# One transpose in place of four: the router's logits and its combine weights in an attention and mixture-of-experts kernel

## What is computed

```
x = x + softmax(mask((ln(x) Wq + bq) (ctx Wk + bk)^T / sqrt(d))) (ctx Wv + bv)
t = ln(x)
scores  = sigmoid(l2norm(t) @ l2norm(gate_w).T)          # 16 logits per token
combine = the 8 largest scores of a token, divided by their sum, 0 elsewhere
routed  = sum over e of combine[:, e] * (silu(t Wg[e]) * (t Wu[e])) Wd[e]
x = x + routed + (silu(t sWg) * (t sWu)) sWd
```

## Time and profile before

| | us |
|---|---|
| three runs | 704.92, 705.00, 705.68 |
| median | 705.0 |
| the profiled execution | 705.73 |
| its span from the first to the last instruction | 703.6 |
| PE busy | 685.5 (97%) |
| PE weight loads busy | 592.4 (84%) |
| DVE, ACT, POOL busy | 461.6, 239.8, 263.0 |

### The profile page before, as it was taken

How to read it: one execution, slowest core, us unless ns; L and a number is a source line. 1 busy time by engine, 2 the same in 40 slices (tenths; PEclk the granted TensorE clock), 3 DMA queues, 4 the chain that set the end, 5 groups by cost and what they waited for, 6 DMA issues and landing times.

```text
span 703.6 us, 10934 instructions
## 1 busy us (share of the span) xinstructions
PE 685.5 (97%) x3995; PEld 592.4 (84%) x3995; DVE 461.6 (66%) x1029; ACT 239.8 (34%) x485; POOL 263.0 (37%) x222
## 2 busy tenths in 40 slices
PE   8997899999999999999999999999999999999997
PEld 6575688888888888888898889888888888888886
DVE  4777656677677766667576766767576775775444
ACT  4545233333424233333323233233333334232221
POOL 2120532534342532525343432525343442434332
PEclk9998799999999999999999999999999999999999
DMA  6326411042110510033110410114100510005100
GB/s 188 113 68 180 157 40 60 1 121 92 61 31 0 182 61 36 26 87 126 60 31 1 182 61 31 30 60 153 61 31 1 182 60 31 2 23 190 61 0 31
DMA packets 32763, 51.18 MB, mean 73 GB/s; under 512 B 3918, under 2 KB 24391, under 8 KB 32711
## 3 DMA queue, kind: packets, MB, share of 16 engines
q1 hardware_dynamic: 32455, 50.23, 21.8%
q10 hardware_dynamic: 256, 0.26, 0.2%
HBM read 46.03 MB, written 4.46 MB: 72 GB/s over the span
## 4 chain that ended last, share of the span: by engine, by line
PE 89%; DVE 3%; DMA 2%; ACT 2%; issue 1%; SPq 1%; POOL 0%; POOLq 0%; DVEq 0%
PE y_ps L295 9%; PE y_ps L297 9%; PE y_ps L296 9%; PE gate_ps L295 9%; PE up_ps L295 9%; PE gate_ps L297 9%; PE gate_ps L296 9%; PE up_ps L297 9%; PE up_ps L296 9%; PE f_ps L383 2%; PE f_ps L405 1%; PE f_ps L416 1%; DMA cb<-c_rows 1%; DMA xin<-in_x_dram 1%; PE up_ps L304 1%
## 5 line engine op out<-in xcount | busy, mean ns | idle before, releaser
L1157 POOL TENSOR_TENSOR hidden<-hidden,cb 128x512 f32<-128x512 f32 x128 | 200.5, 1567 | 300.5 <-DVE hidden L950 250.6
L946 DVE SCALAR_TENSOR_TENSOR hidden<-hidden,gate_ps 128x512 f32<-128x512 f32 x136 | 93.1, 685 | 148.2 <-ACT hidden L663 147.9
L663 ACT ACTIVATE hidden<-gate_ps 128x512 f32<-128x512 f32 x136 | 81.4, 599 | 271.1 <-PE gate_ps L297 271.1
L295 PE MATMUL y_ps<-W,hs 128*128 128x256 f32 x544 | 156.9, 288 | 6.4 <-ACT hs L670 3.3
L297 PE MATMUL y_ps<-W,hs 128*128 128x256 f32 x544 | 153.9, 283 | 0.0
L296 PE MATMUL y_ps<-W,hs 128*128 128x256 f32 x544 | 153.7, 283 | 0.0
L956 DVE TENSOR_TENSOR hs<-hidden,hs 128x512 fp32r<-128x512 f32 x136 | 97.9, 719 | 27.3 <-ACT hs L670 27.3
L295 PEld LDWEIGHTS y_ps<-W,hs 128*128 128x128 f32 x544 | 102.9, 189 | 12.0 <-ACT hs L670 4.7
L295 PE MATMUL gate_ps<-xT,W 128*128 128x512 f32 x272 | 109.1, 401 | 0.0
L295 PE MATMUL up_ps<-xT,W 128*128 128x512 f32 x272 | 108.8, 400 | 0.0
L297 PE MATMUL gate_ps<-xT,W 128*128 128x512 f32 x272 | 108.6, 399 | 0.0
(11 more groups left out here) (141 smaller groups left out, 721.1 us busy)
## 6 DMA issues: line engine op xcount, KB each, us to landing
cb<-c_rows SPq DMA_DIRECT2D x64, 512.0 KB, 4.2
xin<-in_x_dram SPq DMA_DIRECT2D x8, 512.0 KB, 3.6
out_dram<-x SPq DMA_DIRECT2D x7, 512.0 KB, 7.0
stage<-in_L_ffn_w_gate_dram SPq DMA_DIRECT2D x16, 128.0 KB, 2.2
stage<-in_L_ffn_w_up_dram SPq DMA_DIRECT2D x16, 128.0 KB, 2.4
stage<-in_L_ffn_w_down_dram SPq DMA_DIRECT2D x16, 128.0 KB, 2.6
cb<-in_ctx_dram SPq DMA_DIRECT2D x1, 512.0 KB
out_dram<-x SPq DMA_DIRECT2D x2, 256.0 KB, 2.1
```

The source lines that it names most:

```text
L295: mm(ps, lh, rh, start=first and i == 0, stop=False)
L663: af(ew[:, i, :], gate_ps[i][:], ACT.Tanh, scale=0.5).then_inc(tanh_done, 1)
L946: V_.scalar_tensor_tensor(out=ew[:, i, :], in0=ew[:, i, :], scalar=1.0, in1=gate_ps[i][:], op0=ALU.add, op1=ALU.mult).then_inc(silu_done, 1)
L1157: pg.tensor_tensor(h[:, i, :], ew[:, i, :], cb[:, pair % PLACES, (e - 1) % 2, :], ALU.mult) \
```

## The change

The partition count is used in full. `zT` becomes 128 partitions wide. ACT reads the logits with four copies, each of 32 partitions by 128 columns, which put the four token tiles under each other on the partitions; then one transpose of 128 by 128 turns all four, and the result has the same layout as before. The combine weights, 128 tokens by 64 columns (tile, expert), are turned by one transpose into 64 partitions by 128 tokens; one copy of that shape takes them to SBUF, and the store writes 64 pieces of 128 numbers (512 bytes) in place of 16 rows of 512 numbers, so that `c_rows` in DRAM holds what it held.

```diff
-    assert HALF <= 512 and CT * D + 2 * KD * CKEYS + D <= PLACES * 2 * TOK
+    assert 2 * E * TILES == P and HALF <= 512 and CT * D + 2 * KD * CKEYS + D <= PLACES * 2 * TOK
...
-        zT = sb("zT", [2 * E, TOK])
+        zT = sb("zT", [TILES * 2 * E, D])
...
             def turn_z(b, hf):
                 wait_apart(pe, (z_read, upto(b, hf, 1, 1)))
-                for j in range(TILES):
-                    ins = nc.tensor.transpose(f_ps[0][:, j * 2 * E:(j + 1) * 2 * E], zT[:, j * P:(j + 1) * P],
-                                              ident[0:2 * E, 0:2 * E])
-                ins.then_inc(z_turned, 1)
+                nc.tensor.transpose(f_ps[0][:, 0:TILES * 2 * E], zT[:, 0:P], ident[:]).then_inc(z_turned, 1)

             def turn_c(b, hf):
                 pe.wait_ge(combined, upto(b, hf, 1, 1))
-                for j in range(TILES):
-                    ins = nc.tensor.transpose(f_ps[1][0:E, j * P:(j + 1) * P], cw[:, j, :], ident[:])
-                ins.then_inc(c_turned, 1)
+                nc.tensor.transpose(f_ps[1][0:TILES * E, 0:P], cw.rearrange("p j e -> p (j e)"), ident[:]) \
+                    .then_inc(c_turned, 1)
...
             def read_z(b, hf):
                 act.wait_ge(routed_z, upto(b, hf, 1, 1))
-                af(zT[:], f_ps[0][0:2 * E, :], ACT.Copy).then_inc(z_read, 1)
+                for j in range(TILES):
+                    ins = af(zT[j * 2 * E:(j + 1) * 2 * E, 0:P], f_ps[0][0:2 * E, j * P:(j + 1) * P], ACT.Copy)
+                ins.then_inc(z_read, 1)
...
-                af(cT[0:E, :], f_ps[1][0:E, :], ACT.Copy).then_inc(c_read, 1)
+                af(cT[0:TILES * E, 0:P], f_ps[1][0:TILES * E, 0:P], ACT.Copy).then_inc(c_read, 1)
...
-                act.dma_start(c_rows, cT[0:E, :]).then_inc(c_stored, 16)
+                act.dma_start(c_rows.rearrange("e (j t) -> j e t", j=TILES), cT[0:TILES * E, 0:P]) \
+                    .then_inc(c_stored, 16)
```

## The result

The changed kernel took 700.68 us in the median of 19 runs (697.11 to 710.34), the kernel before 708.10 in the median of 19 beside it (702.83 to 714.62). The ratio is 0.990, with a 95% interval from 0.987 to 0.993: faster, by 5 to 9 us. The profiled execution has a span of 697.5 us, against 703.6 before.

What follows compares the result with a forecast made beforehand. The prediction took PE to bound the loop: 7 x (0.45 + 0.31) = 5.3 us saved, less 0.2 in the start-up, makes 5.1, taking the median of 705.0 to 699.9. The range was 699.0 to 702.7.

Steps and rivals of the forecast that it cites:

- the sum: Whole kernel: 7 x (0.45 + 0.31) = 5.3 us saved, 0.2 given back in the start-up, so 5.1.
- What bounds the kernel: Loop: PE is never idle, 80.14 us per chunk period; what leaves its stream shortens the kernel seven times.
- turn_z: Logits turn on PE: one transpose at 0.11 us replaces a block of 0.56; saves 0.45 per chunk, bounds 0.21 and 0.48.
- turn_c: Combine-weights turn on PE: one transpose at 0.11 us replaces 0.42; saves 0.31 per chunk, bounds 0.29 and 0.34.
- read_z: ACT's logits read: four copies take 0.75 us for 0.59; 0.2 more taken, at most 0.49, paid in the start-up.
- The cover of read_z: Loop: copies end at 137.97, latest 138.26, before the logits transpose can start at about 138.3; hidden by 0.3 or barely.
- The turn of the weights: Wait of the weights transpose for DVE's weights: cover shrinks from 0.54 to 0.09 us, -0.1 at worst; taken as just covered.
- The store: Store of the turned combine weights: 64 pieces land in 1.6 to 2.1 us, 0.5 more at most, inside a cover of 1.4.
- The rival on the slower side: Store of combine weights lands late, past the 1.4 us cover, and PE waits at expert 1's down; 708.3 if 4.2; chance 0.05.
- The entry price stays: Rival at the logits turn: the 0.24 us belongs to its wait or change to transpose; 0.21 saved there, 701.6; chance 0.13.
- PE gets nothing: Rival at both turns: a single transpose between matmuls costs as much as four; 705.2 us; chance 0.04.
- A new wait takes part: Rival at both turns: PE waits for weights or the four copies, losing 0.1 to 0.4 per chunk; 701.7; chance 0.16.

Runs made afterwards that it cites:

- e3_four_full: Kernel before, its four logits transposes kept but each padded to 128 partitions by 128 columns; ratio 1.001, 0.9 us faster at an equal clock.
- e6_six_copies: Changed kernel with two idle copies of 32 by 128 ahead of the four logits copies; one run, 704.46 us.
- e5_late_spread: Changed kernel with an extra 32 KB DRAM copy awaited before the first spread of the combine weights, from the second chunk on; one run, 713.64 us.
- e4_dve_read: Changed kernel with the first chunk's four logits copies made by VectorE in place of ScalarE; ratio 0.993 to the kernel before.
- e8_dve_read_again: Same kernel as e4_dve_read, run again, against the kernel before; ratio 0.990.
- e7_dve_all: Changed kernel with the four logits copies made by VectorE in every chunk; ratio 0.994 to the kernel before.

## Why the prediction was right

It said 699.9 with a range from 699.0 to 702.7, and "faster"; measured were 700.68 in the median, and at an equal clock 4.3 us less, where the sum said 5.1. The way and the mechanism were right; that the median came within 0.8 of 699.9 is in part luck, as the end of this section says. By its steps:

- **What bounds the kernel**: right. The loop is PE's stream: 0.46 and 0.32 us fewer at its two blocks are 0.74 fewer in the period. Where the 0.04 between them goes I didn't find.
- **turn_z, 0.45 saved** with 0.21 and 0.48 as bounds: the block fell by 0.46, the period by 0.42 with this part alone. The reading that the 32 rows carry a price of 0.24 decided between 0.45 and 0.21. `e3_four_full` shows that the wait and the change to a transpose don't carry it; that it is the rows, and not the few moving columns, is argued.
- **turn_c, 0.31 saved**: 0.32 at the block, 0.29 in the period.
- **read_z, 0.2 more, at most 0.5**: mis-sized. It is 0.51 (1.10 for 0.59). The step that failed is the overlap of 0.11 between copies, taken from two copies of the start-up; these four start 0.28 apart and last 0.27. The pair was badly chosen: it goes from one PSUM bank to another (128 partitions, then 26). The next pair in the same trace, L595 and L596, was the nearer one: no overlap, and so 1.08 for four, the prediction's own bound. The start-up pays all of it, 0.5 in place of 0.2, so the sum should have been 7 x 0.74 - 0.5 = 4.7, and 4.3 plus or minus 0.5 was timed.
- **The cover of read_z, "0.3 or barely"**: it was barely, 0.05, and the range held it. Had ScalarE's copies been 0.1 longer, PE would have waited: in `e6_six_copies` 0.56 more cost 0.53.
- **The turn of the weights "just covered"**: right. VectorE's weights end 0.07 before the load that needs them. Counted from the logits (L440, 136.68 before and 135.84 after) they come as late as before, 10.12 for 10.11, and PE's load 0.46 sooner, 10.19 for 10.65: PE has run into them.
- **The store, 1.6 to 2.1, inside its cover**: its path took 2.09 in place of 1.63 and nothing waited. The cover of 1.4 minus that growth is 0.9 to 1.0; the profile has 1.1, and `e5_late_spread` 1.2. The rival on the slower side needed a growth past that cover, and more than the 0.74 gained on top.
- **The entry price stays** and **PE gets nothing** are refuted by the two blocks of 0.10, the first by `e3_four_full` too. **A new wait takes part** did not happen, but it was the near one: both transposes stand within 0.1 us of one.

The range was given for the median of the runs shown first, 705.0. The kernel before had 708.1 in the comparison that followed and 705.3 to 707.6 in those of the experiments; what the profile accounts for, 4.7 of 705 or 0.993, is the edge of the interval of the ratio. Those 19 runs of before have no clock listed, so whether it makes the rest stays open. The medians lie 7.4 apart (708.10 and 700.68) where the sum said 5.1 and the profile accounts for 4.7.

## What to carry to other kernels

In a loop that one engine fills, read what a block costs from the starts of the instructions around it, with and without the block, and not from its durations: that showed a price of some 0.24 us around four small transposes that no row of the loop lists as idle. Four transposes of 32 rows were worth padding to 128: full ones cost 0.11 each where the small ones cost an estimated 0.08, but the price around them went. Stacking them into one was worth more. Work moved to another engine to make that possible (four copies for one) is free only as long as its cover lasts, and where that engine leads, as in the start-up here, it is paid in full.

## What was not expected of the hardware

**Copies out of PSUM that don't overlap.** Four copies of 32 by 128 by ScalarE, which read the same 32 partitions and write four different groups of 32, took 1.10 us (1.09 in `e6_six_copies`), the full 0.27 and a hundredth for each; VectorE's took 0.28 each, 0.29 apart. Others in the same stream overlap by 0.1. In the kernel before, the pairs that copy the same 26 partitions of one PSUM bank to two groups of partitions don't overlap either (L595 and L596, 0.36 long and 0.38 apart; L633 and L634, 0.57 long and 0.59 apart). All of these read one bank twice and change the group of partitions that they write; which of the two makes the difference was not tried.

**The granted clock of the start-up differs between runs of one program.** Busy time by stretch of `e4_dve_read`, and after it of `e8_dve_read_again`, the same program:

```profile
20.00:30.00 10.00, 8.50 (x34) 4.68 (x33) 8.03 (x17) 4.31 (x12) 2.50 (x3) 0.89 0.59 172
30.00:40.00 10.00, 10.00 (x26) 4.71 (x24) 2.29 (x10) 2.15 (x9) 0.00 (x0) 0.50 0.09 27
40.00:50.00 10.00, 10.00 (x52) 7.71 (x52) 6.21 (x18) 3.62 (x7) 0.15 (x1) 0.76 0.00 0
```

```profile
20.00:30.00 10.00, 8.87 (x34) 5.48 (x33) 8.11 (x17) 4.49 (x13) 2.51 (x3) 0.83 0.61 175
30.00:40.00 10.00, 8.81 (x53) 5.65 (x53) 4.75 (x15) 5.55 (x16) 0.00 (x0) 1.00 0.08 25
40.00:50.00 10.00, 10.00 (x75) 8.06 (x74) 8.45 (x23) 3.71 (x8) 3.53 (x6) 1.00 0.15 41
```

In the one the clock stays at half, 1.2 of 2.4 GHz, from 30 to 40 us and PE gets through 26 matmuls in place of 53; its logits come 5.25 us later (57.18 for 51.93). The profile of `e7_dve_all` shows the same 26 matmuls at 0.50 in that stretch. The loop after it runs at 1.00 in both. Between these two runs that is 5.25 of the 6.9 us of the spans (705.5 and 698.6), more than the change is worth; another 1.8 lie between the first and the second chunk's logits, again at different clocks (0.66 and 0.97 from 80 to 90 us). What sets it off was not tried.
